# Summing convolution products on VectorE before the transposes, and a third row buffer, in a gated-convolution and mixture-of-experts kernel

## The chip, the cores and the metric

The kernel runs on one core of one Trainium2 chip. The metric is the time of one execution on the device in microseconds (us); lower is better. The engines are called TensorE (PE in the profile, its weight loads PEld), VectorE (DVE), ScalarE (ACT), GpSimd (POOL) and SyncE (SP, which here only issues DMAs).

## What is computed

Inputs are `x` and `ctx`, both 8 x 256 x 512 in f32 (batch, head row, position), and the weights. There are 32 heads of 8 rows each. The reference, cut to what matters:

```python
# 1: gated long convolution; k = v = ctx, q = layernorm(x)
kv  = einsum('bhil,bhjl->bijhl', ctx, ctx)          # 8 x 8 products of rows of a head
y   = irfft(rfft(kv, 2*L) * rfft(ssm_kernel, 2*L))[..., :L] + kv * D
out = einsum('bijhl,bhil->bjhl', y, q)              # for each j: sum over i of y[i, j] * q[i]
x2  = x + tanh(g_xattn) * out
# 2: mixture of experts on t = layernorm(x2), 2048 rows of 512
scores = softmax(t @ gate_w.T); weights, indices = top_k(scores, 2)   # 16 experts
y = sum over e of swiglu(t, w1[e], w3[e], w2[e]) * w_e; z = swiglu(t, shared)
out = x2 + tanh(g_ffn) * (y + z)
```

`swiglu(t, a, b, o)` is `(silu(t @ a.T) * (t @ b.T)) @ o.T`.

## The kernel before

**Stage one** (to about 208 us) walks over 16 tiles of 128 rows, two heads by 8 rows by 8 batches. The convolution is a triangular Toeplitz product: positions are split in 4 blocks of 128, and for block `lb` `conv(t, lb)` (L1211) multiplies `lb + 1` Toeplitz blocks with the kv products of a tile, for each of the two heads `h`, three matmuls each because every f32 operand is split into a high and a low part. That is 6, 12, 18 and 24 matmuls with 288 columns for `lb` 0 to 3. As kv[i, j] = kv[j, i], only 36 of 64 pairs are made; they come in five groups by distance i - j: 0, 1, 2, 3 (8 rows each) and 4 (4 rows). The two heads of a block land in the two halves of a two-bank PSUM tensor `pair`, of which there are two, used in turn.

`products(t, lb)` (L814) on VectorE multiplies these results by q. For each head there are three instructions: 256 elements of `y * q` into `prod` in SBUF (L830), 192 into the PSUM bank `ps_rows` (L835) and 64 more there (L838). Then one instruction (L842) adds `ps_rows` and the first 512 columns of `prod` into `rows`. `sum_rows(t, lb)` (L1239) on TensorE turns five blocks of 128 columns (four of `rows`, one of `prod`) back into row order by transposes against `ident`, all accumulated into one piece of PSUM bank `ps_o`: the remaining sum over the five groups is made by the accumulation.

The order on each engine is written out by hand in its `turn(t)`:

- TensorE (L1252): conv 0; sum_rows of block 3 of the tile before; conv 1; gate (L1200) of tile t-2; sum_rows 0; conv 2; sum_rows 1; conv 3; turn_t of tile t-1; turn_q of tile t+1; sum_rows 2.
- VectorE (L868): products 0; `residual(t-1)` (L795: x2, its statistics by bn_stats and bn_aggr); logits_copy(t-2); products 1; scale_x2(t-1) and scale_x(t+1), four instructions on one column each; products 2; products 3.
- ScalarE (L669): copies, squares and high parts; statistics of x; `q_copy` (L604), which moves the transposed q from PSUM into `q` in two instructions (L611, L612); `norm_x2`; `tT_copy`.

`conv(t, lb)` waits (`prod_ok`) for the products of the block before, since `pair` is reused two blocks on. `products` waits for `conv_ok`: with count `t*8 + 2*lb + h + 1`, so for each head by itself. Products 0 also wait for `q_ok`.

**Stage two** (from about 210 us) runs 63 tiles of 128 rows in the order of `ORDER`: 10 shared tiles first (meanwhile routing is worked out), then 47 routed ones with four shared ones between them (`MID`, with a buffer `tn_mid` of their own), then two shared ones. A shared tile is two units, a routed one is one: 79 units. In step n TensorE runs `up` of unit n (24 matmuls of 352 columns), three transposes of the hidden rows of unit n-1 (L1312), for a routed tile two ahead `turn_tile` (L1275, transposes at L1186), and `down` of unit n-2 (9 matmuls of 512 columns). ScalarE and VectorE split weights (L734, L741, L1151, L1156), activations and tiles into high and low parts.

The input rows of a tile arrive in `tn[o % 2]`, o the place in `ORDER`. Shared tiles are loaded by SP's queue (`load_rows`, L498), routed ones gathered by GpSimd (`gather`, L1421) with an indirect DMA. `fills_at(n)` (L323) says in which step: tile o + 3 after the last unit of tile o, and tile 2 in step 0. Both wait for `tTl_ok` to reach o - 1, which is when the tile that had the buffer has been split. Tiles 0 and 1 are loaded by SP ahead of its last turn of stage one, tile 2 behind that turn and behind a wait for all of stage one's stores (L514 to L516). On GpSimd's queue the gathers stand between the `add_out`s (L1433), indirect DMAs that add `ys` to the output; each waits for the one before it to have landed (`added`). ScalarE writes `ys` at L722 and waits for the add of two tiles before.

Of the kernel before, what the change touches and what calls it, by code (L numbers as in the profile page):

```python
# [22 lines left out]
F32 = mybir.dt.float32  # L23
# [4 lines left out]
ALU = mybir.AluOpType  # L28
# [11 lines left out]
PRODROWS = 5  # L40
PROD_STEPS = 6
EXPERTS, INTER = 16, 352
# [102 lines left out]
def view(ap, offset, dims):  # L145

    return bass.AP(ap.tensor, ap.offset + offset, [list(ap.ap[0])] + dims)


def program(nc, x, ctx_ext, conv_rows, conv_d, gates, gate_w, weights, out):  # L150
    ctx = ExitStack()
    with ctx:
        def sem(name):
            return ctx.enter_context(nc.semaphore(name))

        def sem2(name):
            return [sem(name + "0"), sem(name + "1")]
# [4 lines left out]
        def sb2(name, shape, dt=F32, stack=ctx):  # L162
            return [sb(name + "0", shape, dt, stack), sb(name + "1", shape, dt, stack)]
# [53 lines left out]
        prod = sb2("prod", [P, PRODROWS * P], F32, one)  # L217
        rows = sb2("rows", [P, L], F32, one)
        spent = sb("spent", [P, L], F32, one)
# [4 lines left out]

        tn = sb2("tn", [P, L])
        tn_mid = sb("tn_mid", [P, L])
# [54 lines left out]
        kvh_first, kvl_first, toep_first = sem("kvh_first"), sem("kvl_first"), sem("toep_first")  # L281
        conv_ok, prod_ok, rows_ok, summed = sem("conv_ok"), sem("prod_ok"), sem("rows_ok"), sem("summed")
        x2_ok, stat2, std2, rstd2, t_ok = sem("x2_ok"), sem("stat2"), sem("std2"), sem("rstd2"), sem("t_ok")
        t_turned, tT_ok, gate_ok, logits_ok = sem("t_turned"), sem("tT_ok"), sem("gate_ok"), sem("logits_ok")
# [6 lines left out]

        tn_in, row_in, tn_mid_in = sem2("tn_in"), sem2("row_in"), sem("tn_mid_in")
        tile_turned, tTh_ok, tTl_ok = sem("tile_turned"), sem("tTh_ok"), sem("tTl_ok")
# [26 lines left out]
        def unit(n):  # L320
            return UNITS[n] if 0 <= n < N_UNITS else None

        def fills_at(n):  # L323

            u, out = unit(n), []
            if n == 0:
                out.append(2)
            if u and u.last:
                out.append(u.o + 3)
            return [o for o in out if o < len(ORDER)]  # L330

# [23 lines left out]
        def tn_count(o):  # L355
            return 16 * sum(ORDER[k][0] == ORDER[o][0] and k not in MID for k in range(o % 2, o + 1, 2))

# [53 lines left out]
        def _(sp):  # L411
# [86 lines left out]
            def load_rows(o):  # L498

                routed, j = ORDER[o]  # L500
                if not routed and o not in MID:
                    wait(sp, tTl_ok, o - 1)
                    sp.dma_start(tn[o % 2][:], tT_t[j]).then_inc(tn_in[o % 2], 16)

            sp.wait_ge(kv_ok, 2 * TILES)
            sp.wait_ge(xn_ok, TILES)
            for p in (0, 1):
                sp.wait_ge(tT_out[p], 16)
            load_rows(0)
            load_rows(1)  # L510
            turn(At(TILES - 1))
# [45 lines left out]
            for o in FINAL:  # L557
                sp.dma_start(tn[o % 2][:], out_t[ORDER[o][1]]).then_inc(final_in, 16)
            for k, o in enumerate(FINAL):
# [6 lines left out]
        def _(act):  # L566
# [37 lines left out]
            def q_copy(t):  # L604

                p = t.odd
                wait(act, prod_ok, (t - 1) * 4 * PROD_STEPS)
                wait(act, q_turned, t + 1)
                src = ps_q[:].rearrange("p (l c) -> p l c", l=BLOCKS)
                dst = q[p][:].rearrange("p (l c) -> p l c", l=BLOCKS)  # L610
                act.activation(dst[:, :, 0:P], src, ACT.Copy).then_inc(q_ok, 1)  # L611
                act.activation(dst[:, :, P:], src[:, :, 0:GROUPS * EXT - P], ACT.Copy).then_inc(q_ok, 1)  # L612

# [79 lines left out]
            def tile_hi(o):  # L693

                routed, i = ORDER[o]
                if routed:
                    act.wait_ge(tile_turned, i + 1)
                    src = ps_t
                elif o in MID:
                    act.wait_ge(tn_mid_in, 16 * (MID.index(o) + 1))  # L700
                    act.wait_ge(up_ok, last_unit(o - 2) + 1)
                    src = tn_mid
                else:
                    act.wait_ge(tn_in[o % 2], tn_count(o))
                    wait(act, up_ok, last_unit(o - 2) + 1)
                    src = tn[o % 2]
                act.activation(tT_hi[o % 2][:], src[:], ACT.Copy).then_inc(tTh_ok, 1)
# [56 lines left out]
        def _(dve):  # L764
# [49 lines left out]
            def products(t, lb):  # L814

                par = lb % 2
                G, HB = GROUPS, HD * BATCH
                for h in range(2):  # L820
                    y = ps_conv[par][:, h * 512:h * 512 + 512]
                    qo = lb * GROUPS * EXT + h * BATCH
                    po = h * BATCH
                    qq, pp = q[t.odd][:], prod[par][:]
                    if h == 0:
                        wait(dve, summed, t * 4 + lb - 1)
                        if lb == 0:
                            wait(dve, q_ok, (t + 1) * 2)
                    wait(dve, conv_ok, t * 8 + 2 * lb + h + 1)
                    dve.tensor_tensor(view(pp, po, [[P + G, 4], [G, HD], [1, BATCH]]),  # L830
                                      view(y, 0, [[HB, 4], [BATCH, HD], [1, BATCH]]),
                                      view(qq, qo, [[0, 4], [G, HD], [1, BATCH]]), ALU.mult).then_inc(prod_ok, 1)
                    if h == 0:
                        wait(dve, rows_ok, t * 4 + lb)
                    dve.tensor_tensor(view(ps_rows, po, [[P, 3], [G, HD], [1, BATCH]]),  # L835
                                      view(y, HB, [[HB, 3], [BATCH, HD], [1, BATCH]]),
                                      view(qq, qo + G, [[G, 3], [G, HD], [1, BATCH]]), ALU.mult).then_inc(prod_ok, 1)
                    dve.tensor_tensor(view(ps_rows, po + 3 * P, [[4 * G, 2], [G, 4], [1, BATCH]]),  # L838
                                      view(y, 4 * HB, [[0, 2], [BATCH, 4], [1, BATCH]]),
                                      view(qq, qo + 4 * G, [[4 * G, 2], [G, 4], [1, BATCH]]), ALU.mult).then_inc(prod_ok, 1)  # L840
                wait(dve, prod_ok, (t * 4 + lb + 1) * PROD_STEPS)
                dve.tensor_tensor(rows[par][:], ps_rows, prod[par][:, 0:L], ALU.add).then_inc(rows_ok, 1)  # L842

# [42 lines left out]
            def tile_lo(o):  # L886
                dve.wait_ge(tTh_ok, o + 1)
                src = ps_t if ORDER[o][0] else tn_mid if o in MID else tn[o % 2]
                dve.tensor_tensor(tT_lo[o % 2][:], src[:], tT_hi[o % 2][:].bitcast(F32),  # L889
                                  ALU.subtract).then_inc(tTl_ok, 1)  # L890
# [283 lines left out]
            for o in FINAL:  # L1174
                dve.wait_ge(down_ok, last_unit(o) + 1)
                dve.scalar_tensor_tensor(ys[o % 2][:], y_bank(o), small[:, 2:3], tn[o % 2][:],
                                         ALU.mult, ALU.add).then_inc(final_ok, 1)
# [3 lines left out]
        def _(pe):  # L1181
# [57 lines left out]
            def sum_rows(t, lb):  # L1239

                if lb == 0:
                    wait(pe, x2_ok, t)
                wait(pe, rows_ok, t * 4 + lb + 1)
                for r in range(PRODROWS):
                    part = (rows if r < BLOCKS else prod)[lb % 2]
                    mm = pe.matmul(ps_o[:, lb * P:(lb + 1) * P], part[:, r * P:(r + 1) * P], ident[:],  # L1246
                                   is_transpose=True, start=(r == 0), stop=(r == PRODROWS - 1))
                mm.then_inc(summed, 1)
# [26 lines left out]
            def turn_tile(o):  # L1275
                pe.wait_ge(row_in[o % 2], tn_count(o))
                wait(pe, tTl_ok, o)
                turn_rows(tn[o % 2], ps_t, tile_turned)

# [83 lines left out]
        def _(pool):  # L1363
# [57 lines left out]
            def gather(o):  # L1421

                routed, i = ORDER[o]
                if not routed:
                    return
                if i == 0:
                    pool.wait_ge(r_done, 1)
                wait(pool, tTl_ok, o - 1)
                pool.indirect_dma_start(out=tn[o % 2][:], out_offset=None, in_=t_rows,  # L1429
                                        in_offset=bass.IndirectOffsetOnAxis(ap=slot_info[:, 3 * i:3 * i + 1], axis=0),  # L1430
                                        bounds_check=ROWS - 1, oob_is_err=False).then_inc(row_in[o % 2], 16)

# [75 lines left out]
```

## Time and profile before

| | us |
|---|---|
| median of 3 runs | 743.13 |
| lowest, highest run | 741.87, 744.69 |
| the profiled execution, its own time | 748.91 |
| its span in the profile | 747.1 |
| TensorE busy in the span | 719.4 |
| VectorE busy | 568.9 |
| ScalarE busy | 459.8 |
| GpSimd busy | 369.6 |

The profiled execution is one execution, 5.8 us above the median of the others; 1.8 us of its time lie outside the span. A row of the timeline gives start, duration, engine, line, operation, operands and a count, and in brackets how long the engine stood idle before it and what released it. The duration of an instruction reaches to its end; a following one can start before that. The chain of waits is followed back from the last instruction; it names what released each step.

### The profile page before, as it was taken

What the parts mean: (1) busy time and instruction counts of PE and PEld (TensorE: products, weight loads), DVE (VectorE), ACT (ScalarE), POOL (GpSimd) and SP (SyncE); (2) the same over time, 40 slices, a digit from 0 to 9 for tenths busy, and PEclk for the clock granted to TensorE, in tenths of its full rate; (3) what the DMA queues carried; (4) which work ended last, traced back from release to release, by engine and by line L of the source; (5) the groups of instructions that cost most, each with busy time, mean ns of one, the idle gap of its engine ahead of it and who ended that gap; (6) DMA issues with size and microseconds to landing.
All of it is one profiled execution on the core that took longest, in us unless ns stands there. A gap on an engine that the chain in (4) does not pass through costs nothing.

```text
span 747.1 us, 15553 instructions
## 1 busy us (share of the span) xinstructions
PE 719.4 (96%) x4602; PEld 677.7 (91%) x4602; DVE 568.9 (76%) x1111; ACT 459.8 (62%) x659; POOL 369.6 (49%) x190
## 2 busy tenths in 40 slices
PE   3999999999999999999999999999989999999998
PEld 3999999999998999899988999888989999999997
DVE  7899989898955578428889588848977689679942
ACT  7575757566432322136978677747976699678941
POOL 4998888886400065032444444334634445434420
PEclk9999999999999999999999999999999999999999
DMA  7678787776522122463567577767655764332101
GB/s 240 221 231 274 222 265 231 256 235 231 171 100 43 29 43 43 141 184 97 164 201 209 124 234 214 178 174 167 159 159 168 170 194 88 73 67 51 29 16 56
DMA packets 48404, 114.88 MB, mean 154 GB/s; under 512 B 7472, under 2 KB 8624, under 8 KB 48336
## 3 DMA queue, kind: packets, MB, share of 16 engines
q1 hardware_dynamic: 35792, 89.67, 36.9%
q0 software_dynamic: 12544, 24.40, 17.3%
q8 instruction: 31, 0.51, 0.3%
q14 instruction: 37, 0.30, 0.1%
HBM read 157.78 MB, written 29.26 MB: 250 GB/s over the span
## 4 chain that ended last, share of the span: by engine, by line
PE 71%; DVE 11%; DMA 8%; issue 5%; ACT 3%; ACTq 1%; DVEq 0%; SPq 0%; POOLq 0%
PE pair L1304 20%; PE bank L1304 15%; PE pair L1329 12%; PE pair L1235 8%; PE bank L1329 7%; DMA out<-ys,slot_info 5%; PE bank L1186 4%; PE pair L1312 3%; PE bank L1246 2%; DVE prod L830 2%; DVE bank L835 2%; DVE x L801 2%; DVE rows L842 1%; DVE st L781 1%; DVE bank L838 1%
## 5 line engine op out<-in xcount | busy, mean ns | idle before, releaser
L1151 DVE TENSOR_TENSOR w_lo<-raw,w_hi 128x1408 fp32r<-128x1408 f32 x94 | 148.6, 1622 | 49.8 <-ACT w_hi L734 49.7
L1442 POOL DMA_INDIRECT out<-ys,slot_info x47 | 83.0, 1765 | 120.7 <-ACT ys L722 85.5
L1429 POOL DMA_INDIRECT tn<-t_rows,slot_info x47 | 77.2, 1643 | 119.6 <-DVE tT_lo L889 87.5
L734 ACT ACTIVATE w_hi<-raw 128x1408 fp32r x94 | 124.6, 1374 | 3.0 <-issue 2.5
L1235 PE MATMUL pair<-kv_hi,toep_hi 128*128 128x288 f32 x320 | 100.6, 314 | 2.0 <-DMA toep_lo<-kpad_lo 1.7
L1235 PE MATMUL pair<-kv_lo,toep_hi 128*128 128x288 f32 x320 | 95.3, 298 | 0.0
L1235 PE MATMUL pair<-kv_hi,toep_lo 128*128 128x288 f32 x320 | 95.2, 297 | 0.0
L1156 DVE TENSOR_TENSOR w_lo<-raw,w_hi 128x1536 fp32r<-128x1536 f32 x47 | 82.4, 1752 | 6.5 <-ACT w_hi L741 6.5
L1380 POOL TENSOR_TENSOR kv_lo<-kv,kv_hi 128x2304 fp32r<-128x2304 f32 x15 | 77.3, 5155 | 6.1 <-ACT kv_hi L626 6.1
L741 ACT ACTIVATE w_hi<-raw 128x1536 fp32r x47 | 69.2, 1473 | 1.5 <-DMA raw<-in_weights 1.1
L830 DVE TENSOR_TENSOR prod<-pair,q 128x256 f32<-128x256 f32 x128 | 53.5, 418 | 15.5 <-PE pair L1235 10.1
L1160 DVE TENSOR_TENSOR hid<-hid,pair 128x352 f32<-128x352 f32 x44 | 22.7, 517 | 55.4 <-ACT hid L748 55.4
L1235 PEld LDWEIGHTS pair<-kv_hi,toep_hi 128*128 128x128 f32 x320 | 61.0, 191 | 2.8 <-DMA toep_lo<-kpad_lo 2.3
L1235 PEld LDWEIGHTS pair<-kv_lo,toep_hi 128*128 128x128 f32 x320 | 61.2, 191 | 0.0
L1235 PEld LDWEIGHTS pair<-kv_hi,toep_lo 128*128 128x128 f32 x320 | 61.0, 191 | 0.0
L374 POOL TENSOR_TENSOR kv<-cx 128x1536 f32<-128x1536 f32 x15 | 52.6, 3506 | 13.9 <-DMA cx<-in_ctx 13.6
L748 ACT ACTIVATE hid<-pair 128x352 f32<-128x352 f32 x43 | 19.5, 454 | 59.3 <-PE pair L1304 59.2
L1442 POOL DMA_INDIRECT out<-ys,own_row x14 | 26.3, 1876 | 59.8 <-ACT ys L722 51.5
L1304 PE MATMUL pair<-w_hi,tT_hi 128*128 128x352 f32 x192 | 46.3, 322 | 2.6 <-DVE w_lo L1151 2.6
L1304 PE MATMUL pair<-w_hi,tT_lo 128*128 128x352 f32 x192 | 46.1, 321 | 0.0
L748 ACT ACTIVATE hid<-bank 128x352 f32<-128x352 f32 x36 | 16.3, 453 | 48.4 <-PE bank L1304 46.6
L1304 PE MATMUL pair<-w_lo,tT_hi 128*128 128x352 f32 x192 | 46.1, 321 | 0.0
(223 smaller groups left out, 2014.7 us busy)
## 6 DMA issues: line engine op xcount, KB each, us to landing
raw<-in_weights SPq DMA_DIRECT2D x94, 704.0 KB
raw<-in_weights SPq DMA_DIRECT2D x47, 768.0 KB
toep_hi<-kpad_hi SPq DMA_DIRECT2D x15, 512.0 KB, 4.5
toep_lo<-kpad_lo SPq DMA_DIRECT2D x15, 512.0 KB, 6.1
cx<-in_ctx SPq DMA_DIRECT2D x15, 384.0 KB, 6.3
stage<-in_weights SPq DMA_DIRECT2D x16, 272.0 KB, 6.6
xt<-in_x SPq DMA_DIRECT2D x16, 256.0 KB, 6.3
xr<-in_x SPq DMA_DIRECT2D x16, 256.0 KB, 6.5
```

The lines of the kernel that those rows point to most:

```text
L374: eng.tensor_tensor(view(z, g0 * k + HB, [[k, g], [HB, 3], [1, HB]]), view(c, g0 * GW, [[GW, g], [0, 3], [1, HB]]), view(c, g0 * GW + BATC ...
L734: act.activation(w_hi[s % 2][:, a:b], raw[:, bass.ds(half + a, b - a)], ACT.Copy).then_inc(hi_ok[n_], 1)
L741: act.activation(w_hi[s % 2][:, W13:WROW], raw[:, bass.ds(half + W13, W2)], ACT.Copy).then_inc(hi_ok[2], 1)
L830: dve.tensor_tensor(view(pp, po, [[P + G, 4], [G, HD], [1, BATCH]]), view(y, 0, [[HB, 4], [BATCH, HD], [1, BATCH]]), view(qq, qo, [[0, 4], ...
L1151: dve.tensor_tensor(w_lo[s % 2][:, a:b], raw[:, bass.ds(half + a, b - a)], w_hi[s % 2][:, a:b].bitcast(F32), ALU.subtract).then_inc(lo_ok[ ...
L1156: dve.tensor_tensor(w_lo[s % 2][:, W13:WROW], raw[:, bass.ds(half + W13, W2)], w_hi[s % 2][:, W13:WROW].bitcast(F32), ALU.subtract).then_i ...
L1235: mm = pe.matmul(ps_conv[lb % 2][:, h * 512:h * 512 + n], w[p][:, k:k + P], z[p][:, o:o + n], start=(mb == 0 and m == 0), stop=(mb == lb a ...
L1304: mm = pe.matmul(dst[:, 0:INTER], a[:, c * P:(c + 1) * P], w[:, f:f + INTER], start=(c == 0 and k == 0), stop=(c == BLOCKS - 1 and k == 2))
L1329: mm = pe.matmul(y_bank(u.o)[:], a[:, c * P:(c + 1) * P], w[:, f0 + c * L:f0 + (c + 1) * L], start=(first and c == 0 and k == 0), stop=(la ...
L1380: pool.tensor_tensor(kv_lo[t.odd][:], kv[t.odd][:], kv_hi[t.odd][:].bitcast(F32), ALU.subtract).then_inc(kvl_ok, 1)
L1429: pool.indirect_dma_start(out=tn[o % 2][:], out_offset=None, in_=t_rows, in_offset=bass.IndirectOffsetOnAxis(ap=slot_info[:, 3 * i:3 * i + ...
L1442: pool.indirect_dma_start(out=out, out_offset=bass.IndirectOffsetOnAxis(ap=rows, axis=0), in_=ys[o % 2][:], in_offset=None, bounds_check=R ...
```

## The change

In stage one the data of a tile is laid out head by head (`x_rows` and the output on the host, `q` in `q_copy`), and `products` is written anew: three multiplications for both heads together (384 elements into `prod`, 128 into `prod`, 512 into `ps_rows`), then three additions of 256 elements: in place in `ps_rows`, from `ps_rows` into a new buffer `half_sum`, and from both into `rows`, which now has 256 columns. `sum_rows` transposes three blocks (two of `rows`, one of `prod`). In stage two `tn` has three buffers, every load or gather is issued one tile earlier, and tile 2 is loaded together with tiles 0 and 1.

```diff
-PROD_STEPS = 6
+PROD_STEPS = 3
+SUMROWS = 2
@@ buffers
-        rows = sb2("rows", [P, L], F32, one)
+        rows = sb2("rows", [P, SUMROWS * P], F32, one)
+        half_sum = sb("half_sum", [P, SUMROWS * P], F32, one)
-        tn = sb2("tn", [P, L])
+        tn = [sb(f"tn{n}", [P, L]) for n in range(3)]
@@ fills_at(n)
-            u, out = unit(n), []
-            if n == 0:
-                out.append(2)
-            if u and u.last:
-                out.append(u.o + 3)
-            return [o for o in out if o < len(ORDER)]
+            def at(o):
+                return max(last_unit(o - 4), 15 if ORDER[o][0] else 0)
+
+            return [o for o in range(3, len(ORDER)) if at(o) == n]
@@ load_rows and gather
-                    wait(sp, tTl_ok, o - 1)
-                    sp.dma_start(tn[o % 2][:], tT_t[j]).then_inc(tn_in[o % 2], 16)
+                    wait(sp, tTl_ok, o - 2)
+                    sp.dma_start(tn[o % 3][:], tT_t[j]).then_inc(tn_in[o % 3], 16)
-            for p in (0, 1):
-                sp.wait_ge(tT_out[p], 16)
-            load_rows(0)
-            load_rows(1)
+            sp.wait_ge(tT_out[0], 32)
+            sp.wait_ge(tT_out[1], 16)
+            for o in range(3):
+                load_rows(o)
-                wait(pool, tTl_ok, o - 1)
-                pool.indirect_dma_start(out=tn[o % 2][:], out_offset=None, in_=t_rows,
+                wait(pool, tTl_ok, o - 2)
+                pool.indirect_dma_start(out=tn[o % 3][:], out_offset=None, in_=t_rows,
@@ q_copy (destination and source by head)
-                act.activation(dst[:, :, 0:P], src, ACT.Copy).then_inc(q_ok, 1)
-                act.activation(dst[:, :, P:], src[:, :, 0:GROUPS * EXT - P], ACT.Copy).then_inc(q_ok, 1)
+                act.activation(view(q[p][:], 0, [[2 * GW, BLOCKS], [GW, 2], [1, HB]]),
+                               view(ps_q, 0, [[P, BLOCKS], [HB, 2], [1, HB]]), ACT.Copy).then_inc(q_ok, 1)
+                act.activation(view(q[p][:], HB, [[2 * GW, BLOCKS], [GW, 2], [1, HB // 2]]),
+                               view(ps_q, 0, [[P, BLOCKS], [HB, 2], [1, HB // 2]]), ACT.Copy).then_inc(q_ok, 1)
@@ products(t, lb), new body
+                y, z, w = ps_conv[par][:], q[t.odd][:], prod[par][:]
+                qo, n = lb * 2 * GW, 4 * HB
+                wait(dve, summed, t * 4 + lb - 1)
+                if lb == 0:
+                    wait(dve, q_ok, (t + 1) * 2)
+                wait(dve, conv_ok, t * 8 + 2 * lb + 2)
+                dve.tensor_tensor(view(w, BATCH, [[n, 2], [HB + BATCH, 3], [1, HB]]),
+                                  view(y, HB, [[512, 2], [HB, 3], [1, HB]]),
+                                  view(z, qo, [[GW, 2], [0, 3], [1, HB]]), ALU.mult).then_inc(prod_ok, 1)
+                dve.tensor_tensor(view(w, 2 * n, [[HB, 2], [HB // 2, 2], [1, HB // 2]]),
+                                  view(y, 4 * HB, [[512, 2], [0, 2], [1, HB // 2]]),
+                                  view(z, qo + HB // 2, [[GW, 2], [HB // 2, 2], [1, HB // 2]]),
+                                  ALU.mult).then_inc(prod_ok, 1)
+                wait(dve, rows_ok, t * 4 + lb)
+                dve.tensor_tensor(view(ps_rows, 0, [[HB, 2], [P, 4], [1, HB]]),
+                                  view(y, 0, [[512, 2], [HB, 4], [1, HB]]),
+                                  view(z, qo, [[GW, 2], [BATCH, 4], [1, HB]]), ALU.mult).then_inc(prod_ok, 1)
                 wait(dve, prod_ok, (t * 4 + lb + 1) * PROD_STEPS)
-                dve.tensor_tensor(rows[par][:], ps_rows, prod[par][:, 0:L], ALU.add).then_inc(rows_ok, 1)
+                m = SUMROWS * P
+                dve.tensor_tensor(ps_rows[:, m:], ps_rows[:, m:], view(w, 2 * HB, [[HB, 2], [n, 2], [1, HB]]),
+                                  ALU.add).then_inc(half_ok, 1)
+                dve.tensor_tensor(half_sum[:], ps_rows[:, 0:m], view(w, 0, [[HB, 2], [n, 2], [1, HB]]),
+                                  ALU.add).then_inc(half_ok, 1)
+                wait(dve, half_ok, (t * 4 + lb + 1) * 2)
+                dve.tensor_tensor(rows[par][:], ps_rows[:, m:], half_sum[:], ALU.add).then_inc(rows_ok, 1)
@@ sum_rows(t, lb)
-                for r in range(PRODROWS):
-                    part = (rows if r < BLOCKS else prod)[lb % 2]
+                last = prod[lb % 2][:, 8 * HB:]
+                for r in range(SUMROWS + 1):
+                    part = rows[lb % 2][:, r * P:(r + 1) * P] if r < SUMROWS else last
```

(`HB` is 64 elements, `GW` 96, `BATCH` 8. Everything that indexed `tn`, `tn_in` or `row_in` by `o % 2` uses `o % 3`.)

## Rows read from the trace of the kernel before

**Rows 1.** Busy time by stretch: stretch, PE, PEld, DVE, ACT, POOL, PEclk, DMA, GB/s.
```profile
100.00:125.00 25.00, 24.74 (x199) 24.27 (x198) 22.73 (x77) 16.22 (x30) 21.80 (x9) 1.00 0.78 243
```

**Rows 2.** Chain of waits: conv 3 of the first and of the sixteenth tile.
```profile
21.30 3.19 PE pair L1235 x24
...
204.95 3.18 PE pair L1235 x24
```

**Rows 3.** Timeline of TensorE, from sum_rows 1 of one tile to the next.
```profile
93.93 0.66 PE L1246 MATMUL bank<-ident,rows 128*128 128x128 f32 x4
...
94.45 0.38 PE L1235 MATMUL pair<-kv_hi,toep_hi 128*128 128x288 f32 x1
...
97.71 0.60 PE L1186 MATMUL bank<-ident,t 128*128 128x128 f32 x4
98.15 0.60 PE L1186 MATMUL bank<-ident,xn 128*128 128x128 f32 x4
...
106.25 0.66 PE L1246 MATMUL bank<-ident,rows 128*128 128x128 f32 x4 [0.18 <-DVE rows L842]
```

**Rows 4.** Timeline of VectorE: end of products 3, products 0, residual, products 1.
```profile
97.91 0.42 DVE L830 TENSOR_TENSOR prod<-pair,q 128x256 f32<-128x256 f32 x1 [0.48 <-PE pair L1235]
...
99.86 0.42 DVE L830 TENSOR_TENSOR prod<-pair,q 128x256 f32<-128x256 f32 x1 [0.39 <-ACT q L612]
100.20 0.36 DVE L835 TENSOR_TENSOR bank<-pair,q 128x192 f32<-128x192 f32 x1
100.46 0.22 DVE L838 TENSOR_TENSOR bank<-pair,q 128x64 f32<-128x64 f32 x1
100.59 0.42 DVE L830 TENSOR_TENSOR prod<-pair,q 128x256 f32<-128x256 f32 x1
...
101.19 0.22 DVE L838 TENSOR_TENSOR bank<-pair,q 128x64 f32<-128x64 f32 x1
101.45 0.69 DVE L842 TENSOR_TENSOR rows<-bank,prod 128x512 f32<-128x512 f32 x1
102.05 0.74 DVE L801 SCALAR_TENSOR_TENSOR x<-bank,small,xr 128x512 f32<-128x512 f32 x1
...
103.91 0.42 DVE L830 TENSOR_TENSOR prod<-pair,q 128x256 f32<-128x256 f32 x1
...
105.50 0.69 DVE L842 TENSOR_TENSOR rows<-bank,prod 128x512 f32<-128x512 f32 x1
...
106.74 0.41 DVE L830 TENSOR_TENSOR prod<-pair,q 128x256 f32<-128x256 f32 x1
```

**Rows 5.** Waits of TensorE: waiter and releaser, total us, times, longest.
```profile
PE bank L1186 <- DMA tn<-t_rows,slot_info: 3.2, 3, 1.9
...
PE pair L1304 <- DVE hid L1160: 1.8, 1, 1.8
```

**Rows 6.** Chain of waits at the start of stage two.
```profile
220.05 2.64 DMA tn<-tT_rows
...
228.52 5.68 PE pair L1304 x24
```

**Rows 7.** Timeline of GpSimd: last constant of the routing.
```profile
222.28 0.14 POOL L1418 IOTA own_row<- 128x16 int32 x1
```

**Rows 8.** Busy time by stretch (columns as in rows 1), behind the wait for tile 2.
```profile
230.00:232.00 2.00, 2.00 (x9) 2.00 (x8) 0.91 (x4) 0.00 (x0) 0.00 (x0) 0.50 0.00 0
```

**Rows 9.** Chain of waits: a unit's `up`, and the longest wait for a gather.
```profile
520.70 3.80 PE pair L1304 x24
...
536.99 9.54 DMA tn<-t_rows,slot_info
```

**Rows 10.** Timeline of GpSimd: the next add to the output behind that wait.
```profile
550.73 1.59 POOL L1442 DMA_INDIRECT out<-ys,slot_info  x1 [5.36 <-DMA out<-ys,slot_info]
```

**Rows 11.** Busy time by stretch (columns as in rows 1), in the middle of stage two.
```profile
450.00:500.00 50.00, 47.72 (x282) 44.15 (x281) 36.89 (x39) 33.14 (x42) 18.85 (x11) 1.00 0.71 191
500.00:550.00 50.00, 45.40 (x263) 41.66 (x262) 42.53 (x41) 39.57 (x47) 23.84 (x13) 0.97 0.68 169
```

More of the change, by code:

```diff
@@ L282, in program @@
         conv_ok, prod_ok, rows_ok, summed = sem("conv_ok"), sem("prod_ok"), sem("rows_ok"), sem("summed")
+        half_ok = sem("half_ok")
         x2_ok, stat2, std2, rstd2, t_ok = sem("x2_ok"), sem("stat2"), sem("std2"), sem("rstd2"), sem("t_ok")
@@ L290, in program @@
         r_fields, r_info, r_done = sem("r_fields"), sem("r_info"), sem("r_done")
-        tn_in, row_in, tn_mid_in = sem2("tn_in"), sem2("row_in"), sem("tn_mid_in")
+        tn_in, row_in = [sem(f"tn_in{n}") for n in range(3)], [sem(f"row_in{n}") for n in range(3)]
+        tn_mid_in = sem("tn_mid_in")
         tile_turned, tTh_ok, tTl_ok = sem("tile_turned"), sem("tTh_ok"), sem("tTl_ok")
@@ L355, in tn_count @@
         def tn_count(o):
-            return 16 * sum(ORDER[k][0] == ORDER[o][0] and k not in MID for k in range(o % 2, o + 1, 2))
+            return 16 * sum(ORDER[k][0] == ORDER[o][0] and k not in MID for k in range(o % 3, o + 1, 3))
         def last_unit(o):
@@ L557, in _ @@
             for o in FINAL:
-                sp.dma_start(tn[o % 2][:], out_t[ORDER[o][1]]).then_inc(final_in, 16)
+                sp.dma_start(tn[o % 3][:], out_t[ORDER[o][1]]).then_inc(final_in, 16)
             for k, o in enumerate(FINAL):
@@ L608, in q_copy @@
                 wait(act, q_turned, t + 1)
-                src = ps_q[:].rearrange("p (l c) -> p l c", l=BLOCKS)
-                dst = q[p][:].rearrange("p (l c) -> p l c", l=BLOCKS)
-                act.activation(dst[:, :, 0:P], src, ACT.Copy).then_inc(q_ok, 1)
-                act.activation(dst[:, :, P:], src[:, :, 0:GROUPS * EXT - P], ACT.Copy).then_inc(q_ok, 1)
+                act.activation(view(q[p][:], 0, [[2 * GW, BLOCKS], [GW, 2], [1, HB]]),
+                               view(ps_q, 0, [[P, BLOCKS], [HB, 2], [1, HB]]), ACT.Copy).then_inc(q_ok, 1)
+                act.activation(view(q[p][:], HB, [[2 * GW, BLOCKS], [GW, 2], [1, HB // 2]]),
+                               view(ps_q, 0, [[P, BLOCKS], [HB, 2], [1, HB // 2]]), ACT.Copy).then_inc(q_ok, 1)
             def tT_copy(t):
@@ L703, in tile_hi @@
                 else:
-                    act.wait_ge(tn_in[o % 2], tn_count(o))
+                    act.wait_ge(tn_in[o % 3], tn_count(o))
                     wait(act, up_ok, last_unit(o - 2) + 1)
-                    src = tn[o % 2]
+                    src = tn[o % 3]
                 act.activation(tT_hi[o % 2][:], src[:], ACT.Copy).then_inc(tTh_ok, 1)
@@ L818, in products @@
                 par = lb % 2
[L819 to L840, printed above, removed]
@@ L887, in tile_lo @@
                 dve.wait_ge(tTh_ok, o + 1)
-                src = ps_t if ORDER[o][0] else tn_mid if o in MID else tn[o % 2]
+                src = ps_t if ORDER[o][0] else tn_mid if o in MID else tn[o % 3]
                 dve.tensor_tensor(tT_lo[o % 2][:], src[:], tT_hi[o % 2][:].bitcast(F32),
@@ L1175, in _ @@
                 dve.wait_ge(down_ok, last_unit(o) + 1)
-                dve.scalar_tensor_tensor(ys[o % 2][:], y_bank(o), small[:, 2:3], tn[o % 2][:],
+                dve.scalar_tensor_tensor(ys[o % 2][:], y_bank(o), small[:, 2:3], tn[o % 3][:],
                                          ALU.mult, ALU.add).then_inc(final_ok, 1)
@@ L1243, in sum_rows @@
                 wait(pe, rows_ok, t * 4 + lb + 1)
-                for r in range(PRODROWS):
-                    part = (rows if r < BLOCKS else prod)[lb % 2]
-                    mm = pe.matmul(ps_o[:, lb * P:(lb + 1) * P], part[:, r * P:(r + 1) * P], ident[:],
-                                   is_transpose=True, start=(r == 0), stop=(r == PRODROWS - 1))
+                last = prod[lb % 2][:, 8 * HB:]
+                for r in range(SUMROWS + 1):
+                    part = rows[lb % 2][:, r * P:(r + 1) * P] if r < SUMROWS else last
+                    mm = pe.matmul(ps_o[:, lb * P:(lb + 1) * P], part, ident[:],
+                                   is_transpose=True, start=(r == 0), stop=(r == SUMROWS))
                 mm.then_inc(summed, 1)
@@ L1275, in turn_tile @@
             def turn_tile(o):
-                pe.wait_ge(row_in[o % 2], tn_count(o))
+                pe.wait_ge(row_in[o % 3], tn_count(o))
                 wait(pe, tTl_ok, o)
-                turn_rows(tn[o % 2], ps_t, tile_turned)
+                turn_rows(tn[o % 3], ps_t, tile_turned)
             def parts(hi, lo, whi, wlo):
@@ L1427, in gather @@
                     pool.wait_ge(r_done, 1)
-                wait(pool, tTl_ok, o - 1)
-                pool.indirect_dma_start(out=tn[o % 2][:], out_offset=None, in_=t_rows,
+                wait(pool, tTl_ok, o - 2)
+                pool.indirect_dma_start(out=tn[o % 3][:], out_offset=None, in_=t_rows,
                                         in_offset=bass.IndirectOffsetOnAxis(ap=slot_info[:, 3 * i:3 * i + 1], axis=0),
-                                        bounds_check=ROWS - 1, oob_is_err=False).then_inc(row_in[o % 2], 16)
+                                        bounds_check=ROWS - 1, oob_is_err=False).then_inc(row_in[o % 3], 16)
             def add_out(o):
@@ L1467 @@
     x, c = a("x"), a("ctx_2048")
-    x_rows = x.reshape(BATCH, TILES, 2, HD, L).transpose(1, 3, 2, 0, 4).reshape(ROWS, L)
+    x_rows = x.reshape(BATCH, TILES, 2, HD, L).transpose(1, 2, 3, 0, 4).reshape(ROWS, L)
     cc = c.reshape(BATCH, TILES, 2, HD, BLOCKS, P)[..., ::-1].transpose(1, 5, 4, 2, 3, 0)
@@ L1506 @@
     got = run(nc, [arrays], core_ids=[0]).results[0]["out_0"]
-    return got.reshape(TILES, HD, 2, BATCH, L).transpose(3, 0, 2, 1, 4).reshape(BATCH, HEADS * HD, L)
+    return got.reshape(TILES, 2, HD, BATCH, L).transpose(3, 0, 1, 2, 4).reshape(BATCH, HEADS * HD, L)
```

## The prediction

> **What bounds the kernel now.** I read four views: busy time by stretch, the waits of TensorE, the chain of waits, then the timeline. In a stretch in the middle of stage one TensorE is busy 24.7 of 25 us and VectorE 22.7, at a granted clock of 1.00 [rows 1]. By that alone TensorE sets the pace. But VectorE is nine tenths full too, and the change takes work from the first and gives it to the second, so the loop has to be followed in the timeline. Conv 3 starts at 21.30 in the first tile and at 204.95 in the sixteenth [rows 2]: 15 periods of 12.24 us.
>
> I measure one period from the start of sum_rows 1, called S, to the next: 93.93 to 106.25, 12.32 us [rows 3]. From S, TensorE needs 0.52 for five transposes, 3.26 for conv 3 and 0.44 each for turn_t and turn_q [rows 3]. ScalarE then copies q, and VectorE starts products 0 at 99.86, released by that copy, after 0.39 idle: S + 5.93. Products 0 take 2.19 (to 102.05), residual and logits 1.86 (to 103.91), products 1 2.28 to the end of `rows` at 106.19, 0.06 before the next S [rows 3, 4]. These sum to 12.32: the loop runs through both engines, and TensorE's next sum_rows 1 stood idle 0.18 for `rows`. VectorE has 0.48 + 0.39 idle in it, since products 3 wait for conv 3 and products 0 for q [rows 4]. So VectorE works 12.32 - 0.87 = 11.4 us of a period, and TensorE has some 0.35 to spare.
>
> **Stage one, TensorE.** A transpose takes 0.44 / 4 = 0.11 [rows 3]. Two go from each of four blocks: 0.88 us a tile less, of which 0.22 (sum_rows 1) lie on the loop above.
>
> **Stage one, VectorE.** Where nothing holds the next instruction, starts follow each other by less than a duration: 256 elements 0.34, 64 elements 0.13, 512 elements 0.60. That is 0.066 us plus 1.04 ns an element. Where the next waits for this one's result, it is duration plus 0.04 (L838 to L842: 0.26 in place of 0.13) [rows 4]. By this the old block is 0.33 + 0.27 + 0.13 + 0.33 + 0.27 + 0.26 + 0.60 = 2.19, as seen. The new one: 384 elements 0.466, 128 elements 0.20, 512 elements 0.69 + 0.035 with a wait behind it, 256 elements 0.333, 256 elements 0.418 + 0.04 with the new wait on `half_ok`, 256 elements 0.333. Sum **X = 2.515 us**, 0.32 more than before: 1792 elements in place of 1536 and one more dependent step outweigh one instruction less. No row shows an addition in place in PSUM; L835 reads PSUM and SBUF and writes PSUM (192 elements, 0.36) and L842 reads the same and writes SBUF, both on one line of cost, so I take that line. Bounds: 2.19 (no dearer than now) and 2.79 (all six at full duration, none overlapped).
>
> **What the new wait holds.** The products now wait for both heads. Products 3 can start only when all of conv 3 is done. S to conv 3 is 0.30 (three transposes), conv 3 to VectorE's start behind it 94.45 to 97.91 = 3.46 [rows 3, 4]: S + 3.76. VectorE would be free at S - 0.15 + 0.63 (four small instructions, 106.11 to 106.74 [rows 4]) + 2.52 = S + 3.0, so it idles 0.76. Then it runs without a gap: products 3, X; products 0, X, as q is ready at about S + 5.7 and VectorE comes only at S + 6.3; residual 1.86; products 1 to the end of `rows`, X + 0.085, and 0.06 to TensorE. Period = 3.76 + 3X + 1.86 + 0.145 = 5.765 + 3X = **13.31 us**. The loop has moved from the path over q to the path over products 3, and TensorE waits twice in it: 0.8 before sum_rows 3 and 1.3 before sum_rows 1. Its saved 0.88 us go into these waits. Check from the other side: VectorE's work is 11.4 + 4 x 0.32 = 12.7, more than 12.24 even with no idle time at all.
>
> Stage one: 15 periods x (13.31 - 12.24) = +16.0. The first tile is paced by its loads and hardly moves. Behind the last conv 3, `rows` of block 3 come 1.0 later, less 0.2 on TensorE: +0.7. **Sum +16.7**; by the bounds of X: 12.35 gives +2.4, 14.1 gives +29.
>
> **What costs nothing.** q_copy writes the same 512 and 256 elements, and q is early now. The host's order of rows moves no byte more. The third `tn` buffer is filled with the first two; tile 2's store (count 32) is long past; its 0.34 us on SP's queue stand ahead of the store of x2, for which SP waits anyway.
>
> **Stage two, the start.** Tile 2's load stood behind the last store, at 220.05. Its split was followed on VectorE by a part of the routing and then by the hidden product for which TensorE waited 1.8 us [rows 5], to start at 228.52 [rows 6]. With tile 2 there, the next thing late is the routing's constant, at 222.42 [rows 7]; the chain of maxima and the hidden product behind it takes as long as before, so `up` of unit 3 starts 1.76 earlier, when TensorE has only just finished. Behind the wait the granted clock was 0.50, 1.2 GHz [rows 8], and 24 matmuls took 5.68 us [rows 6] against 3.80 elsewhere [rows 9]: 1.9 more. Both go: **-3.6**.
>
> **Stage two, the gathers.** Each gather keeps its place on GpSimd's queue and its wait comes true at the same moment (tile o of the old slot and tile o + 1 of the new one wait for the same split), so no add and no transfer moves; it only has a unit's time more before it is needed. Two gathers now stand together in step 15, when the queue is quiet. TensorE waited three times for one, 3.2 us [rows 5]. The longest: 9.54 us of transfer [rows 9] and 1.9 idle, behind which the clock fell: 0.97 over 50 us is 1.5 us lost [rows 11]. That is 3.4 us, but the next add was itself released only at 550.73 [rows 10] and ScalarE's next `ys` hung on the same landing, so I give back 0.9 and take -2.5. At the two others the weights' split came late in the same unit: nothing. So -2.5 in this execution; bounds 0 and -4.7 (all of 3.2 and 1.5).
>
> Sum for an execution like the profiled one: 748.9 + 16.7 - 3.6 - 2.5 = 759.5. That execution lies 5.8 above the median, and such transfer stalls are what differs between executions, so of the -2.5 I carry -1.5 to the median: 743.1 + 16.7 - 3.6 - 1.5 = **754.7**.
>
> **Rivals.**
> - A: the waits between VectorE's instructions cost nothing extra, and only the sum of durations counts: old 2.68 a block, new 2.79 [rows 4], +0.11. X = 2.30, period 12.67, +6.5 with the tail: 744.5. Against it: starts 0.34 apart at a duration of 0.42, and 0.26 against 0.13 with a wait [rows 4]. The Trainium skill, page "VectorE: DVE Perf Modes", section "The DRAIN you can't avoid", says that the next operation can't start before the pipe is empty and that a semaphore costs nothing extra; by that rule the time would be this one. The trace does not bear it out. Chance 0.10.
> - B, the other side: the 64-element runs, where L830 has runs of 8, stream faster. It decides from X = 2.19 down: period 12.35, +2.4, which stage two's gain outweighs. At X = 2.0 the path over q and that over products 3 are both 11.7: 743.1 - 7.4 - 5.1 = 730.6. Against it: L842 reads full runs and lies on the same line of cost [rows 4]. Chance 0.08.
> - C: TensorE's clock falls in stage one behind its new waits. It fell after 1.8 and 1.9 us of idle time [rows 5, 8, 11]; the new waits are 0.8 and 1.3. If the longer one is enough, conv 3, 24 matmuls too, pays 1.9 in each period [rows 6, 9]: 15 x 1.9 = +28, 783. The Trainium skill, page "TensorE: Matmul & The Clock Gate", has the clock fall after idle time and come back with sustained work; rows 8 agree. Chance 0.06.
> - D: the extra lead time of the gathers frees ScalarE and the adds too, and all late units of stage two come back on time. Between 450 and 550 TensorE idled 2.3 + 4.6 us and lost 1.5 to the clock [rows 11]: 743.1 + 16.7 - 3.6 - 8.4 = 747.8, nearer the forecast if the median lacks some of these. Against it: the adds keep place and length. Chance 0.12.
>
> **How the numbers follow.** The forecast keeps 0.64, with a range of its own from 750 to 760. A measurement of this kernel can tell 0.5%, 3.7 us, from no change. Slower by more: the forecast, C, most of D and a little of A, 0.76. Within: most of A, a third of D, the low edge of the forecast, 0.15. Faster: B and a little of D, 0.09. The range reaches down over A and D to 743.5 and up over a dearer X (2.62: +5) to 761; B and C stay outside.
>
> **What would show it.** Right: conv 3 starts about 13.3 us apart; the in-place and the half sums take 0.42 each; VectorE idles some 0.7 before products 3 and not at all before products 0; TensorE waits for `rows` before sum_rows 3 and 1; `up` of unit 3 starts without a wait and at full clock; no wait for a gather. A period near 12.7 would show A, one below 12.3 B, a clock under 1.00 in stage one C. The forecast is wrong if VectorE has a gap before products 0, or if its new instructions leave the line of cost.

## The result, and the profile of the changed kernel

The changed kernel takes 759.88 us (median of 6 runs, 758.0 to 762.48), the kernel before, run again beside it, 743.91 (6 runs, 740.25 to 748.21): ratio 1.0226, 95% interval 1.0194 to 1.0258. It is slower by 16 us, 5 more than the 754.7 that was forecast, and inside the stated range of 743.5 to 761 (at the upper edge of the 750 to 760 that the forecast had for itself). The profiled execution of the change took 758.0, its span is 756.1.

The page of the changed kernel, engines and their busy time:

```profile
PE 708.5 (94%) x4474; PEld 662.3 (88%) x4474; DVE 585.7 (77%) x1047; ACT 459.6 (61%) x659; POOL 369.8 (49%) x190
```

TensorE works 11 us less, VectorE 17 us more. The same stretch of stage one as in [rows 1], and the waits of TensorE and VectorE (waiter and releaser, us in all, times, longest):

```profile
100.00:125.00 25.00, 21.34 (x164) 20.22 (x162) 22.57 (x60) 14.35 (x24) 19.45 (x9) 1.00 0.69 227
...
PE bank L1250 <- DVE rows L845: 22.2, 31, 1.2
...
PE bank L1250 <- DVE x L803: 6.9, 15, 1.0
...
DVE prod L827 <- PE pair L1238: 13.7, 18, 1.2
```

TensorE, busy 24.7 of 25 us before, is now busy 21.3. Over the whole of stage one it waits 29 us for VectorE, in place of 1.8 before. The granted clock stayed at 1.00. In the chain of waits of the change, conv 3 of the first, second and sixteenth tile [answers to rows 2] and unit 4 of stage two, and then the same unit in the kernel before:

```profile
22.02 3.19 PE pair L1238 x24
...
35.19 3.19 PE pair L1238 x24
...
223.12 3.19 PE pair L1238 x24
...
252.80 3.81 PE pair L1308 x24
```

```profile
236.85 3.81 PE pair L1304 x24
```

A period is (223.12 - 22.02) / 15 = 13.41 us, against 12.24. The first `up` of stage two, in the timelines of the change and of before:

```profile
229.76 0.56 PE L1308 MATMUL pair<-shared_hi,tT_hi 128*128 128x352 f32 x2
```

```profile
210.74 0.57 PE L1304 MATMUL pair<-shared_hi,tT_hi 128*128 128x352 f32 x2
```

So the ledger of the two profiled executions is +19.0 at the end of stage one, +15.95 at unit 4 (252.80 against 236.85), and +9.0 at the end of the span. The last step is the one that the medians don't have: their difference is 16.0, close to what stands at unit 4, though their interval alone is 14.4 to 19.2. The profiled execution of before (748.91) was slower than the 743.13 it was first given with and than the six runs above; that of the change (758.0) is as fast as its fastest.

One period on VectorE in the changed kernel, from products 3 on [answers to rows 4]:

```profile
119.25 0.56 DVE L827 TENSOR_TENSOR prod<-pair,q 128x384 f32<-128x384 f32 x1 [0.74 <-PE pair L1238]
119.73 0.28 DVE L830 TENSOR_TENSOR prod<-pair,q 128x128 f32<-128x128 f32 x1
119.92 0.69 DVE L835 TENSOR_TENSOR bank<-pair,q 128x512 f32<-128x512 f32 x1
120.65 0.43 DVE L840 TENSOR_TENSOR bank<-bank,prod 128x256 f32<-128x256 f32 x1
120.99 0.41 DVE L842 TENSOR_TENSOR half_sum<-bank,prod 128x256 f32<-128x256 f32 x1
121.44 0.42 DVE L845 TENSOR_TENSOR rows<-bank,half_sum 128x256 f32<-128x256 f32 x1
121.78 0.55 DVE L827 TENSOR_TENSOR prod<-pair,q 128x384 f32<-128x384 f32 x1
...
124.29 0.74 DVE L803 SCALAR_TENSOR_TENSOR x<-bank,small,xr 128x512 f32<-128x512 f32 x1
...
135.37 0.56 DVE L827 TENSOR_TENSOR prod<-pair,q 128x384 f32<-128x384 f32 x1 [0.28 <-issue]
```

And TensorE over the same period [answers to rows 3]:

```profile
115.41 0.44 PE L1250 MATMUL bank<-ident,rows 128*128 128x128 f32 x2 [0.72 <-DVE rows L845]
...
121.92 0.44 PE L1250 MATMUL bank<-ident,rows 128*128 128x128 f32 x2 [0.78 <-DVE rows L845]
...
125.17 0.43 PE L1250 MATMUL bank<-ident,rows 128*128 128x128 f32 x2 [0.31 <-DVE x L803]
...
128.72 0.44 PE L1250 MATMUL bank<-ident,rows 128*128 128x128 f32 x2 [0.64 <-DVE rows L845]
```

VectorE waits 0.74 for conv 3 and then runs through products 3, products 0, residual and products 1 without a gap; TensorE waits for it before sum_rows 3, 0 and 1. From 115.41 to 128.72 is 13.31. In the looped tiles every second products 0 begin after 0.28 us of idle time that nothing released (the row at 135.37).

### The profile page after: what moved, and what is told of

The parts are those of the page before. It is cut to its first block, busy times and chain, and to the rows that moved or that the text cites. A ratio compares the mean times of both kernels' runs of the same rounds, so it can differ in the third digit from the quotient of the medians.

```text
span 756.1 us, 15198 instructions
## 1 busy us (share of the span) xinstructions
PE 708.5 (94%) x4474; PEld 662.3 (88%) x4474; DVE 585.7 (77%) x1047; ACT 459.6 (61%) x659; POOL 369.8 (49%) x190
## 4 chain that ended last, share of the span: by engine, by line
PE 65%; DVE 18%; DMA 8%; issue 5%; ACT 2%; POOL 1%; DVEq 1%; ACTq 0%; SPq 0%; POOLq 0%
PE pair L1308 19%; PE bank L1308 14%; PE pair L1333 12%; PE pair L1238 8%; DMA out<-ys,slot_info 7%; PE bank L1333 6%; DVE bank L835 4%; PE pair L1316 3%; DVE bank L840 3%; PE bank L1189 2%; DVE half_sum L842 2%; DVE prod L830 2%; DVE prod L827 2%; DVE x L803 1%; DVE st L783 1%
## 5 line engine op out<-in xcount | busy, mean ns | idle before, releaser
L1250 PE MATMUL bank<-ident,rows 128*128 128x128 f32 x128 | 27.2, 295 | 29.1 <-DVE rows L845 22.2
L1250 PEld LDWEIGHTS bank<-ident,rows 128*128 128x128 f32 x128 | 13.9, 142 | 37.7 <-DVE rows L845 32.4
L827 DVE TENSOR_TENSOR prod<-pair,q 128x384 f32<-128x384 f32 x64 | 35.3, 552 | 14.9 <-PE pair L1238 13.7
```

The lines of the kernel that those rows point to most:

```text
L827: dve.tensor_tensor(view(w, BATCH, [[n, 2], [HB + BATCH, 3], [1, HB]]), view(y, HB, [[512, 2], [HB, 3], [1, HB]]), view(z, qo, [[GW, 2], [ ...
```

## Experiments

Kernels before in each group of runs had medians of 742.5 to 744.9, so ratios are the better measure.

**The two halves of the change.** First stage one of the change with the old buffers:

```diff
-        tn = [sb(f"tn{n}", [P, L]) for n in range(3)]
+        tn = sb2("tn", [P, L])
```

(and the issue steps and waits of before).

> The change's stage one with the old stage two (two tn buffers, old issue steps). In the two profiles the first up starts 19.0 us later after the change, and 3.2 us of that are won back by unit 4. My theory: stage one alone costs +19 over before, with a period of 13.3 to 13.7 between two conv 3; 763 against 744. Rival: part of the 19 is the early load of tile 2 on SP's queue or the new addresses of the buffers, and this kernel stays below +16.

Measured: 761.94, ratio 1.0252 (1.0217 to 1.0286), 17 to 19 us more. The period is (222.92 - 21.74) / 15 = 13.41, that of the change. Stage one is the whole of the loss, and the rival is out.

Then the buffers of the change with the old stage one:

```diff
-        tn = sb2("tn", [P, L])
+        tn = [sb(f"tn{n}", [P, L]) for n in range(3)]
```

(with everything of the change's diff that concerns `tn`).

> The third tn buffer with all its earlier loads and gathers, the old stage one. Theory (the start of stage two is the gain, the gathers give nothing in the median): -3.2, ratio 0.996. Rival (the 6.8 us that the two profiles differ by between unit 15 and unit 60 belong to the gathers): -7 to -10, ratio 0.987 to 0.99.

Measured: 740.58, ratio 0.9958 (0.9930 to 0.9985). The rival is out.

And the third buffer for tile 2 alone, every other load and gather with its old step and its old wait:

```diff
             def at(o):
-                return max(last_unit(o - 4), 15 if ORDER[o][0] else 0)
-            return [o for o in range(3, len(ORDER)) if at(o) == n]
+            u = unit(n)
+            return [u.o + 3] if u and u.last and u.o + 3 < len(ORDER) else []
```

> Three tn buffers, but only tile 2 is loaded early; every other load and gather keeps its old step and its old wait. If the start is all there is, the same time as with the buffer alone: -3.2. If the gathers matter, this one is slower than that one by what they are worth. In the profile the wait of up of unit 3 for the hidden product (1.8 us) and the clock of 0.50 behind it are gone in either case.

Measured: 741.94, ratio 0.9961 (0.9941 to 0.9980). What can be measured of the buffer is the early tile 2, about 3 us. TensorE's wait for the hidden product [rows 5] is 0.3 us in both of these profiles and 1.9 in that of stage one alone. Whether the earlier gathers add anything isn't resolved: the medians of the two kernels are 1.4 us apart, their ratios 0.0003, and each ratio is good to some 2 us. The waits of TensorE for a gather, 3.2 us in three before [rows 5], are absent from the profile of the change. They are smaller, but there, in the two kernels that keep two buffers (stage one alone, then both heads, below):

```profile
PE bank L1190 <- DMA tn<-t_rows,slot_info: 1.1, 2, 0.6
...
PE bank L1186 <- DMA tn<-t_rows,slot_info: 0.9, 2, 0.5
```

No kernel with three buffers shows a matmul that waits for a gather, not even that with tile 2 alone, whose gathers are not issued earlier. So the absence can't be put down to the earlier gathers, and the 3.2 us were more than the other two executions had.

**What costs time in stage one.** Only the wait for both heads, in the old kernel:

```diff
-                    wait(dve, conv_ok, t * 8 + 2 * lb + h + 1)
+                    wait(dve, conv_ok, t * 8 + 2 * lb + 2)
```

> The old kernel, with the first product of each block waiting for both heads, nothing else. My recurrence: period 3.98 + 3 x 2.19 + 1.86 + 0.145 = 12.57 by the path over products 3 (0.52 for five transposes in place of 0.30), so +0.3 a tile, +5 in all. Rival: the wait for both heads is the cost of the change's stage one, and this kernel shows most of the 19. Second rival: it costs nothing, since VectorE has idle time there.

Measured: 750.54, ratio 1.0070 (1.0044 to 1.0096), +5.2. Conv 3 of the first and the sixteenth tile, from the chain:

```profile
22.03 3.20 PE pair L1235 x24
...
210.69 3.20 PE pair L1235 x24
```

(210.69 - 22.03) / 15 = 12.58; the recurrence gave 12.57. With the old five transposes and the old products the wait for both heads costs 0.33 a tile of the 1.16 that the change costs. It is under a third of the loss, and both rivals are out.

The same wait taken back where it matters, in products 3 of the changed kernel:

```diff
+                if lb == 3:
+                    by_head(t, y, z, w, qo, n)     # 192, 64 and 256 elements, for each head
+                    return add_up(t, lb, w)        # the three additions as they are
                 wait(dve, conv_ok, t * 8 + 2 * lb + 2)
```

> The changed kernel, but the three multiplications of products 3 are made for each head by itself (192, 64 and 256 elements), the first head's while conv 3 still runs. VectorE's work grows by 0.2 us a tile. If the loop goes over the end of conv 3 and products 3, the first head's 0.73 us fit into the 0.75 us of idle time and 2.51 behind conv 3 become 1.98: period 13.41 - 0.54 = 12.87, -8 us against the changed kernel, about 752. Rival, VectorE is full and nothing but its work counts: +0.2 a tile, 763.

Measured: 753.32, ratio 1.0151 (1.0105 to 1.0197). Conv 3 of the fourth and the sixteenth tile:

```profile
60.70 3.18 PE pair L1264 x24
...
215.29 3.20 PE pair L1264 x24
```

(215.29 - 60.70) / 12 = 12.88, forecast 12.87. VectorE has more work than in the change (busy 48.1 of the 50 us from 50 to 100, against 45.3) and the kernel is some 6 us faster (6.6 by the medians, 5.6 by the ratios): the path over products 3, not the sum of VectorE's work, set the period.

Two transposes more in each block of the changed kernel:

```diff
+                for r in range(2):
+                    pe.matmul(ps_o[:, lb * P:(lb + 1) * P], rows[lb % 2][:, r * P:(r + 1) * P], ident[:],
+                              is_transpose=True, start=True, stop=True)
```

> The changed kernel with two more transposes in front of each block's three, whose result is overwritten. Theory: of the 0.88 us more a tile only the 0.22 in front of conv 3 lie on the loop, the others fall into TensorE's waits: +3.3, 763. Rival, TensorE's work counts in full: +14. Second rival, nothing of it counts: 0.

Measured: 764.82, ratio 1.0300 (1.0254 to 1.0346), 5 above the change, with an uncertainty as large. The profile is sharper:

```profile
35.36 3.19 PE pair L1238 x24
...
226.43 3.20 PE pair L1238 x24
```

(226.43 - 35.36) / 14 = 13.65, against (223.12 - 35.19) / 14 = 13.42 in the change: 0.22 a tile for 0.88 us of added work, 0.22 forecast. The saved transposes had been worth a quarter of what they took.

An addition left out (the one in place in PSUM, so one sum is missing in the result):

```diff
-                dve.tensor_tensor(ps_rows[:, m:], ps_rows[:, m:], view(w, 2 * HB, [[HB, 2], [n, 2], [1, HB]]),
-                                  ALU.add).then_inc(half_ok, 1)
```

> The changed kernel without the addition of 256 elements in place in PSUM (one of the sums is left out of the result). It takes 0.333 of a block on VectorE. If three blocks lie on the loop, the period falls by 1.0 to 12.4: -15, about 745. If VectorE's total sets the pace, four blocks count: -1.33 a tile, -20. If the instruction is cheap or hidden: under -5.

Measured: 752.04, ratio 1.0119 (1.0073 to 1.0165), only 8 below the change. But the period is (207.42 - 33.45) / 14 = 12.43, the 12.4 that was forecast:

```profile
33.45 3.19 PE pair L1236 x24
...
207.42 3.19 PE pair L1236 x24
...
PE bank L1306 <- DVE w_lo L1152: 7.4, 6, 1.9
...
PE pair L1306 <- DVE w_lo L1152: 2.5, 2, 2.0
```

So three blocks of four lie on the loop: 3 x 0.33 = 0.99 less, and 13.42 - 12.43 is 0.99. The rest was lost in stage two, where TensorE now waits 9.9 us for split weights, 2.4 in the profile of the change. With a sum missing, x2 and so the routing are others, and the routed tiles can fall differently on the experts; that this is what makes the weights late was not tested. The expectation compared the whole time, which it should not have; the period is the comparison that holds.

**The long periods.** VectorE's tiles written out in the changed kernel:

```diff
-            pairs(dve, turn)
+            for t in range(TILES):
+                turn(At(t))
```

> The changed kernel with VectorE's own tiles written out instead of looped two by two. In the profile of the change every second period is 13.69 instead of 13.31, with 0.28 us of idle time without a releaser in front of products 0, where the loop turns. Theory: the turn of the loop, hidden before in a wait, is now on the path: all periods 13.31 but for single ones, -2.3 us in the span of stage one. Rival: the longer periods come from a transfer or from ScalarE and stay.

```profile
34.20 3.20 PE pair L1239 x24
...
219.81 3.20 PE pair L1239 x24
```

(219.81 - 34.20) / 14 = 13.26, and single periods lie at 13.25 to 13.27 from the second tile on. From the second to the sixteenth tile that is 2.3 us less than in the change, as forecast. The long ones are gone with the loop. The time, 759.98 with runs from 754 to 763 (ratio 1.0223, 1.0171 to 1.0275), does not resolve 2 us.

**The old loop over q.** The third buffer with the old products, and q turned first:

```diff
-                if not first:
-                    turn_t(t - 1)
                 if not last:
                     turn_q(t + 1)
+                if not first:
+                    turn_t(t - 1)
```

> The old stage one with the third tn buffer, and turn_q ahead of turn_t on TensorE. The old loop runs over the copy of q, which then starts 0.44 earlier: 12.24 - 0.44 = 11.8, less than TensorE's own work of 11.98, so the period is 12.0 and the kernel 3.6 faster than with the buffer alone: about 737. Rival: the old stage one is paced by TensorE and the order of the two transposes changes nothing: 740.6.

A miss: 740.59, ratio 0.9965 (0.9944 to 0.9987), no gain over the buffer alone that the runs resolve; by the chain the period is 12.17 in place of the forecast 12.0. VectorE's row at the start of products 0 tells why:

```profile
99.47 0.42 DVE L829 TENSOR_TENSOR prod<-pair,q 128x256 f32<-128x256 f32 x1 [0.26 <-PE pair L1234]
```

Before, it waited 0.39 for the copy of q [rows 4]; now it waits 0.26 for conv 0, which TensorE runs only after both turns and sum_rows 2. One wait had hidden another 0.1 behind it. So conv 0 was moved as well (that of the first tile stands ahead of the loop):

```diff
             def turn(t):
-                conv(t, 0)
                 if not first:
                     sum_rows(t - 1, 3)
@@ behind conv(t, 3)
                 if not last:
                     turn_q(t + 1)
                 sum_rows(t, 2)
+                if not last:
+                    conv(t + 1, 0)
+                if not first:
+                    turn_t(t - 1)
```

> The third buffer, the old products, and TensorE's order after conv 3: turn_q, sum_rows 2, conv 0 of the next tile, turn_t. With turn_q first alone, VectorE waited 0.26 us for conv 0 in place of q and the period was 12.17. Now conv 0 is done before q is there: the loop over q is 11.9, and TensorE's work of 11.98 sets the period at 12.0: -2.5 against 740.6, 738. Rival: another wait comes up (rows for sum_rows 1, or kv for conv 0, since ScalarE's copy of t is later) and the period stays at 12.15.

Measured: 738.77, ratio 0.9932 (0.9898 to 0.9965), faster than both kernels: by 5 us than the old and by 21 than the new one. Against the buffer alone (0.9958) the times don't resolve the gain; the period does. Its chain, and busy time by stretch:

```profile
33.29 3.18 PE pair L1234 x24
...
200.10 3.19 PE pair L1234 x24
...
100.00:125.00 25.00, 25.00 (x205) 24.90 (x204) 23.36 (x77) 17.17 (x29) 23.07 (x10) 1.00 0.81 256
```

(200.10 - 33.29) / 14 = 11.92, forecast 12.0. TensorE is busy all 25 of 25 us: it sets the pace here.

> The same with stage one's tiles written out on TensorE, VectorE, ScalarE and GpSimd instead of looped. If the turns of the loops are on the path there too, up to -2 more; if TensorE is the pace and its loop turns behind its queue, nothing.

Here `pairs` wrote out all 16 tiles, one after the other. Measured: 739.37, ratio 0.9932 (0.9905 to 0.9960), no difference; the period is (200.72 - 34.43) / 14 = 11.88 in place of 11.92. With TensorE setting the pace, the turns of the loops cost next to nothing here.

## Why the prediction was right

The sign, the mechanism and the place were right: the loop went over to the path through products 3, and the runs above bear out each part of it. The size was 5 us short (a change of 16.0 against 11.6). By its own steps:

- **The block.** X was put at 2.515 us from one line of cost. The starts at 119.25, 121.78 and 124.29 give 2.53 and 2.51. The addition in place in PSUM, which no row had shown, takes 0.43 for 256 elements, like the others. Rivals A and B fall here: additions without a wait start 0.34 apart at a duration of 0.43, and with the wait on `half_ok` 0.45 apart.
- **The period.** 13.31 was forecast, with VectorE idle 0.76 before products 3 and not before products 0. Measured are 13.31 with 0.74 idle in one looped tile of two, and 13.7 in the other. That the first agrees to the hundredth is in part luck: conv 3 to VectorE's start took 3.53 for 3.46, and residual and logits 1.77 for 1.86. The missed term is the turn of VectorE's own loop, which the sum had at nothing. In the kernel before, each products 0 of the loop waits 0.36 to 0.39 for q, so the turn probably lay inside that wait; writing out VectorE's tiles was tried in the changed kernel only. The mean is 13.41: 15 periods cost 17.45 (201.10 - 183.65) where 16.0 was put.
- **The tail and the first tile.** From conv 3 of the last tile to the first `up` it is now 229.76 - 223.12 = 6.64, before 210.74 - 204.95 = 5.79: +0.85, forecast +0.7. The first conv 3 stands 0.7 later. But it stands at 21.30 before, at 20.53 with the buffer alone and at 21.69 with tile 2 alone, three kernels with the same stage one, so 0.7 is within what executions differ by. Stage one: 19.0 measured, 16.7 forecast.
- **A wait that was overlooked.** sum_rows 0 waits for x2 of the tile before, 6.9 us in 15 waits. The forecast had two waits, 0.8 before sum_rows 3 and 1.3 before sum_rows 1; there are three, 0.78, 0.31 and 0.64. The one more cost nothing, as TensorE waits again before sum_rows 1.
- **The start of stage two.** -3.6 forecast, -3.1 measured at unit 4, and 3 us by the ratios of both kernels with the old stage one and the buffer. `up` of unit 3 comes 1.5 earlier, not 1.76, and takes 4.15 in place of 5.68, not the 3.80 that was put, at a granted clock of 1.00 from 246 to 250. What was named as next late is what is late now:

```profile
246.00 4.15 PE pair L1308 x24
...
246.00 0.59 PE L1308 MATMUL pair<-shared_hi,tT_hi 128*128 128x352 f32 x2 [0.29 <-DVE hid L1163]
...
DVE texp L1115 <- POOL own_row L1422: 0.9, 1, 0.9
```

- **The gathers.** -1.5 was carried to the median. The runs resolve no gain, and can't exclude one of this size. The term was read from a single execution whose waits for gathers (3.2 us) were longer than in the other two profiles with two buffers (1.1 and 0.9), so taking only a part of it was right.
- **The rest.** 17.45 + 0.85 - 3.1 + 0.7 = 15.9, up to rounding the ledger at unit 4. These terms come from two single executions, so that the medians' 16.0 agrees so closely is in part luck. By this sum, of the 4.4 us between forecast and measured change 1.45 are the loop's turn, 1.5 the gathers, 0.7 the first tile, 0.5 the start and 0.15 the tail. The loop's turn and the start were tested by runs of their own; the other three are read from the rows or argued.
- **Rival C** did not come: the granted clock was 1.00 all through the loop, with waits of 0.3 to 0.8 us in the period above. The wait of 1.3 on which it rested did not occur there (the longest of the waits for VectorE was 1.2). Nor does a longer one suffice by itself: in stage two of the change TensorE stood idle for 1.97 us, more than the 1.8 and 1.9 behind which the clock fell before, and it stayed at 1.00:

```profile
519.13 0.56 PE L1308 MATMUL pair<-w_hi,tT_hi 128*128 128x352 f32 x2 [1.97 <-DVE w_lo L1154]
...
519.00:521.00 2.00, 1.87 (x12) 1.90 (x13) 2.00 (x4) 2.00 (x3) 1.12 (x1) 1.00 0.68 168
```

- **Rival D** did not come either: the buffer with all its gathers gained 3 us, not 12. (Rival A's +6.5 is short of its own tail: 15 x 0.43 and some 0.6 are 7.0. Nothing hangs on it.)

The Trainium skill, page "VectorE: DVE Perf Modes", section "The DRAIN you can't avoid", says that a semaphore between two operations costs nothing extra. The rows of the change differ on that: the same 256 elements occupy 0.34 us without a wait behind them and 0.45 with one. The section also says that a next operation that is not held starts earlier, and the 0.34 at a duration of 0.43 agree with that. By the forecast's own figures the change would take some 10 us less if the wait were free and only durations counted (rival A, 744.5 against 754.7), and the measurement sides with the rows.

## What to carry to other kernels

When work moves from an engine that looks full to one that looks nearly as full, follow one period of the loop through both engines before adding up busy time. Here 0.88 us taken from TensorE gave 0.22. Of the 1.3 us given to VectorE some 1.0 counted, because three of its four blocks stand one behind the other on the path over products 3, and the wider wait that closed this path cost another 0.33. Together, 1.0 + 0.33 - 0.22, that is the 1.1 us a tile that was forecast; with the turn of the loop it became 1.16. A wait that is removed is worth only the distance to the next one behind it, so look up what that engine waits for next (q, then conv 0), and take a gain that rests on one late transfer from several executions, not from one.

## What the hardware showed that was not expected

The turn of VectorE's own loop shows in front of an instruction as 0.28 us of idle time without a releaser and makes the period about 0.4 us longer, once in two tiles. It disappeared when the tiles were written out (13.26 in place of a mean of 13.42). In the kernel with TensorE busy all the time, writing out the tiles on all four engines changed the period by 0.04 us and the time by nothing that could be measured.

Idle time of nearly the same length was followed by a fallen clock in one kernel and not in the other: 1.8 and 1.9 us of it before (the clock was 0.50 from 230 to 232 [rows 8] and 0.97 from 500 to 550 [rows 11]), 1.97 us in the change, with 1.00 behind it. What makes the difference was not tested.
